# Attention with the values stationary on TensorE, division deferred, and a quarter of the full units multiplied whole in fp32

## The reference

```python
q, k, v = (x @ Wq, x @ Wk, x @ Wv)          # B 2, T 2048, C 256, 16 heads of 64
q, k = rmsnorm(q, q_rms_w), rmsnorm(k, k_rms_w)
gate = softplus(einsum('bthd,hd->bht', k, u / |u|) / 8)
bias = -dist * softplus(omega) * slope * gate[key]        # causal, else -inf
y = softmax(q @ k.T / 8 + bias) @ v
x = layernorm(x + y @ Wproj)
h = silu(x @ w1.T * s1) * (x @ w2.T * s2)                 # hidden 1024
h = gelu(h @ h1.T * s);  h = gelu(h @ h2.T * s)
out = layernorm(x + h @ w3.T * s3)
```

## Time and profile before

| | us |
|---|---|
| median of 3 runs | 3840.42 (3836.8 to 3847.71) |
| the profiled execution | 3829.98, span 3828.2 |
| attention up to the first scores | 158 |
| attention from there | 2605 |
| ffn_up | 580 |
| ffn_down | 486 |

### The profile page before, as it was taken

The page is one execution under the profiler, slowest core; times in us unless marked ns, Lnnn a source line. Parts: engine busy times, 40 slices in busy tenths (PEclk is TensorE's granted clock), DMA queues, the critical chain, the costliest instruction groups (busy, mean ns, idle before and its releaser), DMA issues. The chain is left out here.

```text
span 3828.2 us, 58077 instructions
## 1 busy us (share of the span) xinstructions
PE 3582.7 (94%) x23600; PEld 3206.4 (84%) x23600; DVE 1931.5 (50%) x4396; ACT 1408.1 (37%) x2367; POOL 469.8 (12%) x290
## 2 busy tenths in 40 slices
PE   3799999999999999999999999999899999899999
PEld 2698888988888898888889888898778888778887
DVE  3556666556665655666655666656233122133232
ACT  1244444444444444444444344444333232232222
POOL 3112111112111111211111211111000000000000
PEclk9899999999999999999999999999899999999999
DMA  1110011110001111001110001110121111130110
GB/s 54 34 26 20 21 22 28 27 23 21 20 21 30 44 37 54 21 20 26 27 27 21 20 21 25 28 25 17 52 87 36 53 45 50 45 128 34 66 67 17
DMA packets 116121, 137.66 MB, mean 36 GB/s; under 512 B 39568, under 2 KB 72464, under 8 KB 115856
## 3 DMA queue, kind: packets, MB, share of 16 engines
q1 hardware_dynamic: 115856, 133.96, 13.0%
HBM read 54.22 MB, written 29.36 MB: 22 GB/s over the span
## 5 line engine op out<-in xcount | busy, mean ns | idle before, releaser
L766 PEld LDWEIGHTS ps_v<-values,exps 128*128 128x128 f32 x8704 | 1133.2, 192 | 146.8 <-ACT exps L478 78.5
L766 PE MATMUL ps_v<-values,exps 128*128 128x65 f32 x8704 | 1149.8, 272 | 48.2 <-DVE y_tok L684 45.2
L478 ACT ACTIVATE exps<-ps_s,bias 128x512 f32<-128x512 f32 (+3 forms) x1280 | 797.5, 623 | 869.2 <-PE ps_s L754 555.9
L666 DVE TENSOR_REDUCE maxes<-ps_m 128x1 f32<-128x512 f32 x768 | 529.1, 689 | 313.4 <-PE ps_m L802 305.0
L802 PE MATMUL ps_m<-k_ext,q_max 128*128 128x512 f32 (+3 forms) x1280 | 538.4, 434 | 59.5 <-DVE maxes L666 56.3
L753 PE MATMUL ps_s<-q_twice,k_split 128*128 128x512 f32 (+3 forms) x1280 | 496.7, 388 | 0.0
L754 PE MATMUL ps_s<-q_ext,k_ext 128*128 128x512 f32 (+3 forms) x1280 | 470.3, 367 | 0.0
L663 DVE CUSTOM_DVE_ANT_0 ps_m<-ps_m,mask_row 128x128 f32<-128x128 f32 (+3 forms) x512 | 254.1, 496 | 244.4 <-PE ps_m L802 242.2
L729 PE MATMUL ps_p<-w_hi,xt_hi 128*128 128x194 f32 x1024 | 294.3, 287 | 25.6 <-POOL w_lo L411 20.3
L802 PEld LDWEIGHTS ps_m<-k_ext,q_max 128*128 128x128 f32 x1280 | 241.6, 195 | 82.7 <-issue 47.7
L488 ACT ACTIVATE raw<-ps_p 128x386 f32<-128x386 f32 x256 | 126.2, 493 | 438.7 <-PE ps_p L729 438.7
(11 more groups left out here) (186 smaller groups left out, 5391.8 us busy)
## 6 DMA issues: line engine op xcount, KB each, us to landing
q_twice<-q_max SPq DMA_DIRECT2D x256, 128.0 KB, 2.3
k_split<-k_ext SPq DMA_DIRECT2D x128, 128.0 KB, 2.2
hidden<-gelu SPq DMA_DIRECT2D x64, 256.0 KB, 2.0
a_in<-hidden SPq DMA_DIRECT2D x8, 2048.0 KB, 10.5
x_rows<-in_L_attn_x_dram SPq DMA_DIRECT2D x16, 256.0 KB, 2.9
acc<-in_L_attn_x_dram SPq DMA_DIRECT2D x2, 2048.0 KB, 9.9
attended<-acc SPq DMA_DIRECT2D x8, 512.0 KB, 2.9
x_tok<-attended SPq DMA_DIRECT2D x8, 512.0 KB, 4.0
```

The costliest lines, as they stand in the source:

```text
L478: nc.scalar.activation(exps[:, u_ % PR, off:QB], ps_s[u_ % 2][:, off:QB], ACT.Exp, bias=bias[slot][:, kt, qb:qb + 1]).then_inc(ex_done, 1)
L666: nc.vector.tensor_reduce(maxes[:, qt, kc:kc + 1], ps_m[v % 2][:, 0:width], AX.X, ALU.max).then_inc(mx_free, 1)
L766: last = nc.tensor.matmul(ps_v[:, t * (D + 1):(t + 1) * (D + 1)], exps[:, u_ % PR, t * P:(t + 1) * P], values[second][:, kt, :], start=(kt ...
```

## The change

The heads are taken in pairs. Per pair one projection of 392 columns stands in the place of two of 194, on half as many matmuls. In a unit the values (66 columns) are now stationary and up to 512 exponentials are moved past them, into one of two banks `ps_v`, with the result transposed (65 rows, 512 queries). There are two kinds of unit (`mode_of`). In 26 of the 40 ("P": 18 full ones, and on the diagonal those of 512 and 384 queries) ACT takes the exponential twice, once rounded to fp32r (`e_hi`) and once in fp32 (`e_all`), GpSimd makes the difference `e_lo` (`take_rest`), and PE makes three fp32r products: `v_main` and `v_rest` with `e_hi` at step `values`, `v_main` with `e_lo` two units later at step `values rest`. In the other 14 ("F": 6 full ones, the diagonal's 256 and 128) ACT takes it once and PE multiplies `v_full` and `e_all` in fp32. DVE copies the undivided result and its sums (`take`) and SP stores them; the sums are read back, inverted and stored. `ffn_up` loads both, multiplies them on GpSimd, splits them on ACT and DVE and multiplies with `Wproj` on PE (`project_y`), the next block's in the first four tiles of the second layer; `attention` has no output product and no `acc` any more. The row of negative maxima comes from one transpose per query block and a DMA (`row_in`) in place of four matmuls. GpSimd's squares and powers are cut into eight each per pair (128x512 and 128x8) and placed as below; at `gate a` and `norm` DVE works on both heads at once.

```diff
+E_RING, HI_RING, LO_RING, Q_RING = 3, 4, 3, 3
...
+def mode_of(v):
+    qb, kt = UNITS[v]
+    if kt - TQ * qb >= TQ // 2:
+        return "F"
+    return "F" if kt < TQ * qb and kt % TQ == TQ - 1 else "P"
...
+        for t in range(TT):
+            at(t0 - 1.68 + 0.036 * t, "project", p, t)
+        for i in range(8):
+            at(t0 - 1.09 + 0.025 * i, "square", p, i)
+        at(t0 - 0.88, "mean", p)
+        for i in range(8):
+            at(t0 - 0.87 + 0.025 * i, "power", p, i)
+        at(t0 - 0.66, "gate a", p)
...
+        for i in range(8):
+            at(t0 - 0.63 + 0.01 * i, "norm", p, i)
+        for i in range(GATE_PARTS):
+            at(t0 - 0.55 + 0.01 * i, "gate b", p, i)
...
+            for i in range(5):
+                at(first + 0.01 + 0.05 * i, "values in", n, i)
+            turns = [first + 0.005 + 0.033 * i for i in range(NTURN)]
+            for i, when in enumerate(turns):
+                at(when, "turn", n, i)
+            start, end = (turns[1] + 0.03, t0 + 0.28) if s == 0 else (t0 + 0.29, t0 + 1.29)
+            for v, (qt, kc) in enumerate(MAXES):
+                qb = qt // TQ
+                when = max(start + (end - start) * v / (NM - 1), turns[2 * qb + 1] + 0.03)
+                at(when, "max", n, v)
...
+            steps.append(("scores", n, v))
...
+        if LAG <= u < HEADS * NU + LAG:
+            steps.append(("values", *divmod(u - LAG, NU)))
+        if u >= LAG_LO:
+            n, v = divmod(u - LAG_LO, NU)
+            if MODES[v] != "F":
+                steps.append(("values rest", n, v))
...
+        def take_rest(eng, on, n, v):
+            u_ = NU * n + v
+            qb, kt = UNITS[v]
+            off = max(0, kt - TQ * qb) * P
+            i = count_of("PD", u_)
+            eng.wait_ge(hi_done, i + 1)
+            eng.wait_ge(ex_done, u_ + 1)
+            if i >= LO_RING:
+                eng.wait_ge(pv_lo, i + 1 - LO_RING)
+            on.tensor_tensor(e_lo[:, i % LO_RING, off:QB], e_all[:, u_ % E_RING, off:QB],
+                             e_hi[:, i % HI_RING, off:QB].bitcast(F32), ALU.subtract).then_inc(lo_by[MODES[v]], 1)
...
-                        nc.gpsimd.tensor_tensor(k_tok[:, :, 0:D], raw[:, :, CK:CK + D], raw[:, :, CK:CK + D], ALU.mult)
-                        nc.gpsimd.tensor_tensor(q_tok[:, :, 0:D], raw[:, :, CQ:CQ + D], raw[:, :, CQ:CQ + D], ALU.mult).then_inc(sq_done, 1)
...
+                    nc.gpsimd.tensor_tensor(sq[:, i % 4, :, :], raw[:, rows, col:col + D], raw[:, rows, col:col + D], ALU.mult).then_inc(sq_done, 1)
...
+                    nc.gpsimd.tensor_tensor(rs[:, i // 2, rows], mean_sq[:, i // 2, rows], power[:, rows], ALU.pow).then_inc(rs_done, 1)
...
+                    if i < 2:
+                        nc.gpsimd.tensor_tensor(v_main[s][:, rows, 0:D], v[:, rows, :], one[:, 0:1].unsqueeze(2).broadcast_to([P, HT, D]), ALU.mult).then_inc(v_hi, 1)
+                    elif i < 4:
+                        gp.wait_ge(v_hi, 2 * n + i - 1)
+                        nc.gpsimd.tensor_tensor(v_rest[s][:, rows, 0:D], v[:, rows, :], v_main[s][:, rows, 0:D].bitcast(F32), ALU.subtract).then_inc(v_done, 1)
+                    else:
+                        nc.gpsimd.tensor_tensor(v_full[s][:, :, :, 0:D], v.rearrange("p (g t) d -> p g t d", t=TQ)[:, :, TQ // 2:, :],
+                                                one[:, 0:1].unsqueeze(2).unsqueeze(3).broadcast_to([P, NQB, TQ // 2, D]), ALU.mult).then_inc(v_done, 1)
+                if step[0] == "values":
+                    n, v = step[1:]
+                    if MODES[v] == "P":
+                        take_rest(gp, nc.gpsimd, n, v)
...
-                        nc.scalar.activation(exps[:, u_ % PR, off:QB], ps_s[u_ % 2][:, off:QB], ACT.Exp,
-                                             bias=bias[slot][:, kt, qb:qb + 1]).then_inc(ex_done, 1)
...
+                    if MODES[v] != "F":
+                        i = count_of("PD", u_)
+                        if i >= HI_RING:
+                            before = split_units[i - HI_RING]
+                            act.wait_ge(pv_hi, before + 1)
+                            rest_taken(act, before)
+                        nc.scalar.activation(e_hi[:, i % HI_RING, off:QB], ps_s[u_ % 2][:, off:QB], ACT.Exp, bias=by).then_inc(hi_done, 1)
+                    if u_ >= E_RING:
+                        before = u_ - E_RING
+                        if MODES[before % NU] == "F":
+                            act.wait_ge(pv_hi, before + 1)
+                        else:
+                            rest_taken(act, before)
+                    nc.scalar.activation(e_all[:, u_ % E_RING, off:QB], ps_s[u_ % 2][:, off:QB], ACT.Exp, bias=by).then_inc(ex_done, 1)
...
-                        nc.vector.reciprocal(recip[:], pv[:, :, D]).then_inc(rc_done, 1)
-                        dve.wait_ge(rc_done, NQB * n + qb + 1)
-                        nc.vector.tensor_tensor(y_tok[:, qb * TQ:(qb + 1) * TQ, second * D:(second + 1) * D],
-                                                pv[:, :, 0:D], recip[:].unsqueeze(2).broadcast_to([P, TQ, D]), ALU.mult).then_inc(y_done, 1)
...
+                    dve.wait_ge(pv_hi, units_before(n, qb))
+                    dve.wait_ge(pv_lo, count_of("PD", units_before(n, qb)))
+                    if grp >= 2:
+                        dve.wait_ge(y_out_done[grp % 2], 16 * (grp // 2))
+                    nc.vector.tensor_copy(y_out[:, grp % 2, :], ps_v[grp % 2][0:D + 1, :]).then_inc(y_done, 1)
...
-                        for t in range(max(0, kt - TQ * qb), TQ):
-                            last = nc.tensor.matmul(ps_v[:, t * (D + 1):(t + 1) * (D + 1)],
-                                                    exps[:, u_ % PR, t * P:(t + 1) * P],
-                                                    values[second][:, kt, :],
-                                                    start=(kt == 0 and t == 0), stop=(kt == TQ * qb + t),
-                                                    skip_group_check=True)
-                        last.then_inc(pv_done, 1)
...
+                    if kt == 0 and grp >= 2:
+                        pe.wait_ge(y_done, grp - 1)
+                    if MODES[v] == "F":
+                        pe.wait_ge(ex_done, u_ + 1)
+                        nc.tensor.matmul(bank[0:VCOLS, off:QB], v_full[s][:, kt // TQ, kt % TQ - TQ // 2, :], e_all[:, u_ % E_RING, off:QB],
+                                         start=False, stop=kt == TQ * (qb + 1) - 1, skip_group_check=True).then_inc(pv_hi, 1)
+                    else:
+                        i = count_of("PD", u_)
+                        pe.wait_ge(hi_done, i + 1)
+                        nc.tensor.matmul(bank[0:VCOLS, off:QB], v_main[s][:, kt, :], e_hi[:, i % HI_RING, off:QB], start=kt == 0, stop=False,
+                                         skip_group_check=True)
+                        nc.tensor.matmul(bank[0:VCOLS, off:QB], v_rest[s][:, kt, :], e_hi[:, i % HI_RING, off:QB], start=False, stop=False,
+                                         skip_group_check=True).then_inc(pv_hi, 1)
...
+                    rest_taken(pe, u_)
+                    nc.tensor.matmul(ps_v[(n * NQB + qb) % 2][0:VCOLS, off:QB], v_main[s][:, kt, :], e_lo[:, i % LO_RING, off:QB],
+                                     start=False, stop=kt - TQ * qb == TQ // 2 - 1, skip_group_check=True).then_inc(pv_lo, 1)
...
+            def first_x(i):
+                for c in range(OC):
+                    split_y(i, c)
+                normalise_x(i)
+                turn_x(i)
...
+            def project_y(i, c):
+                m = OC * i + c
+                pe.wait_ge(ylo_done, m + 1)
+                if c == 0:
+                    pe.wait_ge(wp_done, 2)
+                    pe.wait_ge(l1_free, 2 + OC * i)
+                for t in range(NT):
+                    out = ps_1[t // 2][:, t % 2 * C:(t % 2 + 1) * C]
+                    tok = slice(t * P, (t + 1) * P)
+                    for j, (y, w) in enumerate(((y_hi, wp_hi), (y_hi, wp_lo), (y_lo, wp_hi))):
+                        last = nc.tensor.matmul(out, y[:, m % 2, tok], w[:, c, :], start=c == 0 and t % 2 == 0 and j == 0,
+                                                stop=c == OC - 1 and j == 2, skip_group_check=True)
+                last.then_inc(y_used, 1)
...
-                    if o == 3 and more:
+                    if o < OC // 2 and more:
+                        project_y(i + 1, 2 * o)
+                        project_y(i + 1, 2 * o + 1)
+                    if o == TURN and more:
                         turn_x(i + 1)
```

More of the change, by code:

```diff
@@ L153, in attention @@
         q_max = [sb(f"q_max{i}", [P, T], F32R) for i in range(2)]
+        q_twice = [sb(f"q_twice{i}", [P, QB], F32R) for i in range(Q_RING)]
         bias = [sb(f"bias{i}", [P, TT, NQB]) for i in range(2)]
@@ new lines, in attention, with units_before, k_cols @@
+        sums_in = [sem(f"sums_in{i}") for i in range(2)]
+        sums_done = sem("sums_done")
```

(27 more changed lines are left out.)

1187 lines of the change are left out of this document (609 added, 578 removed).

## The result

The changed kernel takes 3926.04 us (median, 3920.43 to 3928.37) against 3844.07 us for the kernel before on the same chip: ratio 1.0213, 95% interval 1.0192 to 1.0234. The prediction was 3735 us, between 3600 and 3900, and faster. It was wrong on both counts. The profiled execution has a span of 3926.6 us (3828.2 before), so 98.4 us have to be found; it takes 3928.4 us, 203.4 more than the 3725 of my sum.

The account below looks back on a forecast made before the run. What PE issues was taken to bound the kernel: pairs of heads fall from 163.6 to 147.6 us (-256 over 16), start +16, attention's end +5, `ffn_up` +130, giving 3725 us profiled, 3735 median; range 3600 to 3900.

Parts of the forecast that it names:

- the 3725 of my sum: Whole kernel, profiled execution: 3829.98 + 16 - 256 + 5 + 130 = 3725 us.
- What bounds the kernel before: Attention before the change: what PE issues sets the time, its waits are little; a pair of heads takes 163.6 us.
- PE's list after: PE's changed work in attention, priced by steps between starts: 34.6 us a head after, 45.8 before.
- the one pair of records: Two PE records at 1608.38 lasting 0.33 us, from which a 512-column fp32 multiply was priced at 0.88 us.
- the 137.6 us a pair that I called the list: Attention: 163.6 us a pair less 22.4 of PE work and 3.6 of removed waits, before new waits.
- GpSimd's queue from the squares to the last power, 7 us: Attention, 19 units: GpSimd has 34.4 us against PE's 23.5; with 4 us absorbed, 7 us surface per pair.
- the ten units with turns: Attention: ACT, PE and DVE about level there, bound by semaphores and one bank `ps_t`; 3 us a pair.
- slower: GpSimd's queue: Rival in attention: GpSimd steps before differences delay `values rest`, lateness is not caught up; 3943 us at 20 surfaced; chance 0.17.
- Both rivals on the fp32 price: Rivals: PE's wide fp32 multiply costs 1.72 us, kernel 3975, chance 0.03; or 0.47 us, kernel 3615, chance 0.07.
- 16 equal savings: Attention: each of 16 pairs goes from 163.6 to 147.6 us, 16.0 less; -256 in all.
- Start: +29 for +16: Before the first scores: two heads' serial preparation adds time, partly offset by work moved later; +16 us.
- `ffn_up`: +163 for +130: `ffn_up`: output products +80.5, a 3.8 us gap per block +27, exposed first block +22; together +130 us.

Follow-up runs that it names:

- e1: Changed kernel with the roots left out: GpSimd multiplies where it raised to a power; 3758.7 us, ratio to before 0.981.
- e3: Changed kernel with the differences of units 2 to 16 in each pair's second head on VectorE instead of GpSimd; 3792.6 us, ratio 0.9901.
- e9: Changed kernel with units 14 to 26 of every second head full instead of split; 3750.1 us, ratio 0.9758.
- e5: Changed kernel, order of steps only: squares and powers begin sooner and spread out, gate and norms 0.14 heads sooner; 3913.4 us, ratio 1.0197.
- e7: Changed kernel, ends only: `ffn_up` output products one output later, constant rows written behind the first weights; 3855.0 us, ratio 1.005.
- e8: Changed kernel with all units full, the list of steps of e5 and both ends of e7; 3580.2 us, ratio 0.933.
- e2: Changed kernel with all 40 units full, no `e_hi`, no difference, two copies of the values; 3689.6 us, ratio 0.9631.

## Why the prediction was wrong, step by step

- **What bounds the kernel before, and PE's list after: right.** Wide fp32 was taken at 0.88 us by the one pair of records, and is 0.855; P products, projections and maxima step as costed. But the 137.6 us a pair that I called the list still held 3.8 us of waits of the kernel before, for maxima and turns (43.0 and 10.6 us from 190 to 2500 us). Without them 133.8; with the 19.6 us of waits that the trace of the changed kernel names, 153.4. PE works 13.4 us of each pair at half clock where it was 2.7, for which I had no term; at twice the time there that is 5.4 us more, an estimate (no run changed the clock alone): 158.8 of the 160.3.
- **GpSimd's queue from the squares to the last power, 7 us: right in the main** (4.8 us of waits for `e_lo` there, 1.6 at the turns, which e1 leaves as they are; a difference takes 1.28, a power 1.64). The runs without roots, with VectorE's differences and with full units in the window take 11 to 13 us off GpSimd and give 9 to 12 back, more than the 7 I let surface: with the waits goes part of the half clock, and in e3 and e9 most of the turns' wait.
- **The step that failed: "in the ten units with turns ... I put 3 us a pair on it".** The ordinary waits of the turns are 3.8. But I let the turns begin on time, and never walked the chain that ends before them on VectorE: last power, gate, eight norms, softplus, listed in 0.22 heads. When it begins PE has 10.8 us of units left, and it takes 19.2 (means of eight pairs). The wait is 8.3 us a pair, 129.7 us in 15 waits. What made it so long is GpSimd beside it: each norm takes 1.42 instead of 0.69 and the gate's second multiply 1.22 instead of 0.19; in all the chain takes 7.7 us more than the 11.5 of the first pair, nearly the whole wait (e9: 13.6 against 10.8, and the wait goes to 2.9). The last power sets the chain's start in the changed kernel, but not the wait: in e1 the chain begins 2.1 us after it and the wait stays at 7.8; and an earlier place in the list (e5) gave nothing in all. I priced the power, the difference and the wait of PE for `e_lo`, but no norm, and took VectorE's other durations from a kernel in which GpSimd idled 88% of the time. The other term at nothing is the half clock, 5.4 us a pair by the estimate above.
- **The rival that came nearest** is the second one, "slower: GpSimd's queue", which gave 3943 us at 20 us surfaced a pair. That it meets 3926 is in part luck: besides the turns' own 3.8, 14.8 us surfaced (6.5 and 8.3), the half clock added some 5, and outside the steady part came 46 us that it did not have. Its mechanism was half right: PE stands less at `values rest` than at the turns behind VectorE, which GpSimd slows not by its queue but by working beside it. Both rivals on the fp32 price are refuted by 0.855.
- **The pair as unit.** I took 16 equal savings; there are 15 steps of 160.3 (160.1 as a mean, for 164.5) and a last pair with nothing to prepare: 105 us for 133. That helped by 12 us.
- **Start: +29 for +16.** The first projection begins at 77.5 us, 34 later than before; I had put 18 on the constants of two heads. e7 moves them behind the weights, and 31 us go.
- **`ffn_up`: +163 for +130.** The products (11.5 us a block) and the gap (3.55) were right. Missing were the half clock behind the gap, 2.3 us for seven blocks, and by difference some 18 us in the first block, where PE waits 11.7 us for one `y_lo` and 6 for the sum, at clock 0.74. e7 took the gap and the clock with it: 41.6 us, for 7 x 5.85.
- **Slips of the sum**: 96 x 0.11 is 10.6, 56.1 / 16 is 3.5, 8.5 + 11.0 + 3.8 is 23.3, and a difference of 1.12 us would take 1.9 us a pair off, not 3. None changes the forecast by more than 0.3 us a pair.

What stays open: why e5 gives back all that its shorter wait gains, beyond that VectorE and the ring of `e_all` are late in turn; and why e8's pair (141.0, with 4.5 us of waits and no half clock) is some 3 us under what the account above gives for it (133.8 less 1.3 of half clock before, with 7.4 for the full units and 4.5 of waits, 144.4).

## What to carry to other kernels

Where a change fills an engine that idled before, don't only add up its new work: take again the durations of the engine that works beside it, and walk each chain that crosses both up to the next wait of the bounding engine. An average of 44% busy hid a stretch of 30 us in each 160 in which GpSimd was busy 28.7, and behind it a chain on VectorE that took 19 us instead of 11.5. And price a saving by the whole trade: one fp32 multiply was dearer for PE than three split ones by 0.15 us, and still better, as it needs no second exponential and no difference (no run parts the two); all units full is 3.7% faster than the kernel before (e2), and 6.7% with both ends and the earlier gates (e8).
